# Causal maxima of the first attention scores: the mask moves from TensorE's products to VectorE's maxima

## The reference

```
attn = jnp.einsum('bqhd,bkhd->bhqk', q, k) * scale
causal = jnp.tril(jnp.ones((S, S), dtype=bool))
attn = jnp.where(causal, attn, jnp.float32(-jnp.inf))
attn = jax.nn.softmax(attn, axis=-1)
out = jnp.einsum('bhqk,bkhd->bqhd', attn, v).reshape(B, S, C)
```

## Time and profile before

| | us |
|---|---|
| timed runs, median (lowest, highest) | 3667.57 (3660.76, 3667.74) |
| the profiled execution, its own time | 3655.43 |
| its span, on which all times below count | 3653.7 |
| TensorE busy over the span | 3193.2 (87%) |
| VectorE busy over the span | 2187.1 (60%) |
| ScalarE busy over the span | 1428.5 (39%) |
| mask products of the first scores, L2572 | 512 |
| maxima, L2664 | 128, 188.0 us busy |

### The profile page before, as it was taken

How to read it: one execution, slowest core, us unless ns; L and a number is a source line. 1 busy time by engine, 2 the same in 40 slices (tenths; PEclk the granted TensorE clock), 3 DMA queues, 4 the chain that set the end, 5 groups by cost and what they waited for, 6 DMA issues and landing times.

```text
span 3653.7 us, 86956 instructions
## 1 busy us (share of the span) xinstructions
PE 3193.2 (87%) x35518; PEld 2230.1 (61%) x35518; DVE 2187.1 (60%) x4820; ACT 1428.5 (39%) x3328; POOL 936.6 (26%) x851
## 2 busy tenths in 40 slices
PE   5689988888988888898868889776999999999998
PEld 5367665666666666666757767665545555554553
DVE  7566777566678666678346645635435545545444
ACT  1534443444443444344136622134433433333241
POOL 0112221412222512231406536341221231220110
PEclk7898998898998989899679989898989999999999
DMA  6111210411111301211348755384111111111000
GB/s 238 41 36 46 65 44 28 128 32 60 51 52 48 122 20 54 60 51 35 100 151 204 183 157 144 103 285 145 23 43 45 47 35 47 41 30 41 1 18 18
DMA packets 224087, 280.89 MB, mean 77 GB/s; under 512 B 35072, under 2 KB 172464, under 8 KB 223312
## 3 DMA queue, kind: packets, MB, share of 16 engines
q1 hardware_dynamic: 184448, 216.93, 18.4%
q0 software_dynamic: 34896, 54.20, 6.7%
q10 hardware_dynamic: 4352, 4.20, 0.3%
HBM read 184.64 MB, written 90.62 MB: 75 GB/s over the span
## 4 chain that ended last, share of the span: by engine, by line
PE 67%; DVE 16%; ACT 5%; issue 4%; DMA 3%; POOL 2%; DVEq 0%; ACTq 0%; SPq 0%; POOLq 0%
PE banks L3020 6%; PE banks L570 5%; DVE s_d_kq L663 4%; PE banks L2586 3%; PE banks L1936 3%; PE banks L2570 2%; PE banks L1278 2%; PE banks L806 2%; PE banks L1945 2%; PE banks L2598 2%; PE banks L966 2%; PE banks L2738 2%; PE banks L794 2%; PE banks L2828 2%; PE banks L964 2%
## 5 line engine op out<-in xcount | busy, mean ns | idle before, releaser
L570 PE MATMUL banks<-s_d_xT,s_w_qkvg 128*128 128x512 f32 x640 | 342.0, 661 | 15.9 <-DVE s_d_kq L663 11.4
L663 DVE SCALAR_TENSOR_TENSOR s_d_kq<-banks,s_conv_w,s_d_kq 128x511 f32<-128x511 f32 (+2 forms) x384 | 286.0, 745 | 49.9 <-ACT s_d_kq L615 40.3
L2700 ACT ACTIVATE s_g_pT<-banks 128x1536 f32<-128x1536 f32 (+1 forms) x96 | 152.8, 1591 | 361.0 <-PE banks L2588 361.0
L2664 DVE TENSOR_REDUCE s_g_nmax<-banks 128x4 f32<-128x512 f32 (+3 forms) x128 | 188.0, 1490 | 162.8 <-PE banks L2572 162.8
L3020 PE MATMUL banks<-s_m_we,s_m_tT 128*128 128x512 f32 x512 | 235.0, 604 | 8.1 <-DVE s_m_x L3084 7.8
L641 ACT ACTIVATE s_d_square<-banks 128x128 bf16<-128x128 f32 x512 | 134.0, 275 | 161.5 <-PE banks L599 161.5
L570 PEld LDWEIGHTS banks<-s_d_xT,s_w_qkvg 128*128 128x128 f32 x640 | 125.8, 208 | 115.8 <-issue 89.4
L615 ACT ACTIVATE s_d_kq<-banks,s_conv_w 128x512 f32<-128x512 f32 x128 | 87.8, 686 | 271.1 <-PE banks L570 270.5
L1936 PE MATMUL banks<-s_q_xsT,s_q_w 128*128 x1008 | 159.9, 282 | 38.4 <-issue 27.5
L1936 PEld LDWEIGHTS banks<-s_q_xsT,s_q_w 128*128 128x128 f32 x1008 | 153.7, 196 | 61.1 <-issue 49.1
L806 PEld LDWEIGHTS banks<-s_d_TB,s_d_XT 32*32 32x32 f32 x9216 | 111.1, 112 | 89.0 <-issue 41.9
(11 more groups left out here) (411 smaller groups left out, 7588.1 us busy)
## 6 DMA issues: line engine op xcount, KB each, us to landing
s_q_w<-w12p SPq DMA_DIRECT2D x128, 257.0 KB, 6.3
s_q_xs<-xs SPq DMA_DIRECT2D x32, 516.0 KB, 6.4
s_d_E<-sums SPq DMA_DIRECT2D x64, 256.0 KB, 3.6
s_r_xT<-xfT SPq DMA_DIRECT2D x12, 1024.0 KB
tree<-s_r_bias SPq DMA_DIRECT2D x96, 128.0 KB, 2.2
s_r_work<-xf SPq DMA_DIRECT2D x24, 512.0 KB, 4.4
og<-s_d_o SPq DMA_DIRECT2D x16, 512.0 KB, 3.0
sorted<-s_q_acc SPq DMA_DIRECT2D x32, 256.0 KB, 2.1
```

What stands on the lines that cost most here:

```text
L570: ins = e.matmul(bk[6 + j % 2][:], w[:, par, c, self.COL[what] + h * P:self.COL[what] + (h + 1) * P], xT[:, c, :], start=(c == 0), stop=(c ...
L663: e.scalar_tensor_tensor(d[:, a:], bk[6 + j % 2][:, 0:SEQ - a], cw[:, par, k0 + 3 - a:k0 + 4 - a], d[:, a:], ALU.mult, ALU.add).then_inc(s ...
L2664: e.tensor_reduce(self.nmax[:, t, :].rearrange("p (k d) -> p k d", k=4)[:, :, 16], psum[:, 0:4, a:a + (t + 1) * P], AX.X, ALU.max, negate= ...
L2700: e.activation(self.pT[c][:], psum[:, 0:4, 0:self.COLUMNS[c]], ACT.Exp).then_inc(self.exped, 1)
```

## The change

The four mask products of a tile go away; the score products close their group themselves. VectorE gets a new tile `off` with one maximum for each head, and a semaphore `off_made`. For tiles 1 to 3 it reduces the 128 t columns left of the diagonal block into `off`, for all four heads at once. Then, for each head of each tile, one `tensor_tensor_reduce` adds the mask to the diagonal block, writes the sum back over the block in PSUM, and takes its maximum, starting from `off` (from -1e30 in tile 0), into `nmax`. `nmax` now has the maximum's own sign, so the queries' addition becomes a subtraction. An unused set of semaphores is dropped.

```diff
@@ -2567,9 +2568,7 @@
         for t, a in self.MAXIMA[u]:
             W = (t + 1) * P
             for k in range(4):
-                ins = e.matmul(bk[k][:, a:a + W], qkT[32 * k:32 * k + 16, j, t * P:(t + 1) * P], qkT[32 * k:32 * k + 16, 4, 0:W], start=True, stop=False, skip_group_check=True)
-            for k in range(4):
-                ins = e.matmul(bk[k][:, a + t * P:a + (t + 1) * P], self.g.identb[:], self.g.neglb[:], start=False, stop=True, skip_group_check=True)
+                ins = e.matmul(bk[k][:, a:a + W], qkT[32 * k:32 * k + 16, j, t * P:(t + 1) * P], qkT[32 * k:32 * k + 16, 4, 0:W], start=True, stop=True, skip_group_check=True)
         ins.then_inc(self.scored, 1)
@@ -2661,7 +2660,16 @@
                     for t, a in units:
-                        e.tensor_reduce(self.nmax[:, t, :].rearrange("p (k d) -> p k d", k=4)[:, :, 16], psum[:, 0:4, a:a + (t + 1) * P], AX.X, ALU.max, negate=True).then_inc(self.maxed, 1)
+                        if t:
+                            e.tensor_reduce(self.off[:, t, :], psum[:, 0:4, a:a + t * P], AX.X, ALU.max).then_inc(self.off_made, 1)
+                    for t, a in units:
+                        if t:
+                            e.wait_ge(self.off_made, 3 * (m + 1) + t)
+                        for k in range(4):
+                            block = g.bank[k][:, a + t * P:a + (t + 1) * P]
+                            lower = self.off[:, t, k:k + 1] if t else -1e30
+                            ins = e.tensor_tensor_reduce(block, block, g.neglb[:], 1.0, lower, ALU.add, ALU.max, self.nmax[:, t, 32 * k + 16:32 * k + 17])
+                        ins.then_inc(self.maxed, 1)
@@ -2684,7 +2692,7 @@
                     e.wait_ge(self.max_turned, m + 2)
-                    e.tensor_tensor(q, turns[:], q, ALU.add).then_inc(self.q_made, 1)
+                    e.tensor_tensor(q, q, turns[:], ALU.subtract).then_inc(self.q_made, 1)
```

More of the change, by code:

```diff
@@ L71, in __init__ @@
         self.stored = [self.sems(f"side_store{n}") for n in range(4)]
-        self.on_tensor, self.on_vector, self.on_scalar, self.on_gpsimd = (self.sems("side_" + n) for n in ("tensor", "vector", "scalar", "gpsimd"))
+        self.on_tensor, self.on_vector, self.on_scalar = (self.sems("side_" + n) for n in ("tensor", "vector", "scalar"))
     def sem(self, name):
@@ L2315, in __init__ @@
         self.oT, self.rden = sb("g_oT", [P, SEQ]), sb("g_rden", [P, TPB, 4])
+        self.off, self.off_made = sb("g_off", [P, TPB, 4]), g.sem("second_off_made")
         self.at, self.aoT = two("g_at", [P, TPB, DIM]), sb("g_aoT", [P, KC, 256])
```

## The result

In the comparison that goes with the forecast the changed kernel took 3639.41 us (median of 5 runs) against 3660.76 of the kernel before (5 runs): ratio 0.9942, 95% interval 0.9923 to 0.9961. Two later comparisons gave 0.9997 [0.9966, 1.0027] and 0.9974 [0.9954, 0.9994]. The three differ among themselves by more than their intervals allow, so a mean of them says little: by whole times the change is worth something between nothing and 0.6%. The sign rests on the stage itself.

What follows compares the result with a forecast made beforehand. TensorE was taken as the bound. Masks saved 34 us, steady-stretch waits for longer maxima cost 34, the ends 8 and the clock 2: +10 us on 3667.57, so 3677.6 us, range 3649 to 3725 (8 in 10).

Steps and rivals of the forecast that it cites:

- The bound: Second layer's stage: TensorE, busy 1047.12 of 1103.70 us, sets the pace; its saved work saves time unless another engine is late.
- The masks: TensorE's mask products: 128 groups at 0.33 us; 4.3 us a stretch remain, 34 us over eight, give or take 13.
- The price of the pair: VectorE's pass plus read-out for each head: 0.34 us start to start, bounded by 0.27 and 0.49.
- rival 1: VectorE's pair is short, 0.27 us: stalls of 2.0 us a stretch, kernel 12 us faster, 3655; chance 0.25.
- The waits: TensorE waiting for longer maxima in six units of a steady stretch: 4.2 us a stretch, 34 us over eight.
- Ends: Waits for maxima ahead of the first exponentials, in the first round A and near the end: +8 us.
- The clock: Longer waits around the low-clock stretch in the stage's first round A: 2 us added to the sum.
- Rival 3: Clock falls in the steady stretches too, 2.5 us in each of eight, 20 us on top: 3698; chance 0.11.
- The median: Whole kernel: +10 us added to the earlier median of 3667.57 us, giving 3677.6.

Runs made afterwards that it cites:

- E1: The kernel before without its 512 mask products, old maxima kept, causal mask left out of them: ratio 0.9962 to before, steady stretch 128.81 us.
- E2: The changed kernel with the 512 mask products put back on TensorE, so VectorE's part alone: ratio 1.0086 to before, steady stretch 134.20 us.
- E7: The changed kernel with one of a tile's four mask products left in: single time 3657.5 us, stretch 131.87 us without a fall of the clock.
- E9: The changed kernel with the head-wise pass made one without a maximum read-out: one execution 3648.89 us, steady stretch 129.55 us.
- E6: The changed kernel with a small 128x1 copy ahead of each of the 512 pairs: ratio 1.0055 to before.
- E8: The changed kernel with masks and single reduces kept in the first round, rounds A's unit 0 and rounds C's unit 2: ratios 0.9972 and 0.9949 to before.
- E5: The changed kernel with the pass of tiles 1 to 3 writing into the neighbour head's bank: one execution 3671.75 us, steady stretch 130.20 us.

## Why the prediction was wrong

**The bound, right.** TensorE sets the pace; what is taken off it counts except where VectorE comes last. E1 and E2 show both halves.

**The masks, too dear by a fifth.** The term was 0.33 a group, 5.28 us a stretch and 4.3 after 0.99 was taken off for A0 and D2. Measured: 0.18 for a single group, 0.72 for unit 0's two, 4.3 for all sixteen and 3.21 in E1, where A0 and the new wait for GpSimd take their share. No row of the trace before said that the 3.49 behind four masks would become 3.63; that took the changed kernel, and its cause E7. The range of 0.1 a group either way held it. Put right alone, this term would have made the forecast slower still.

**The price of the pair, the step that failed.** "My value is the sum nearest to a row: 0.27 + 0.07 = 0.34." Measured 0.27, and 0.25 with a constant, the low bound and rival 1's value. Rival 1's number is partly luck: it was made up of a pass of 0.20 and a read-out of 0.07, and with the scalar, as in three of four pairs, the pass alone takes 0.26 (E9). Both rows were read rightly: L759's 0.27 is a pass with a scalar (0.26 in E9), and a small instruction costs 0.07 (E6's copy adds 0.06 to 0.07). But two overheads that each stand in a row by themselves were added, the scalar's 0.06 and the read-out's 0.05, and together they cost 0.07. Of the 0.07 by which 0.34 was too high, 0.04 is this overlap (0.20 + 0.06 + 0.05 = 0.31 against 0.27); the rest is the pass taken at 0.27 for 0.26 and the read-out at 0.07 for 0.05. So the maxima grew by 0.94 (0.60 + 4 x 0.25 + 4 x 0.27 + 0.08 = 2.76 against 1.82) and by about 0.66 in units 1 and 2, not by 1.59, 0.94 and 0.95. At 0.33 to 0.34, in E6, the steady stretch has 0.3 us of its gain left and the kernel was slower as a whole, so this step decides whether there is a gain at all.

**The waits, right in place, too long by that step.** Forecast 4.2 us a stretch in A0, B0, C0, C2, D0 and B2; measured 0.24 in B0, 0.33 in C2, 0.61 + 0.11 on the two sides of A0, on top of the masks lost there, and about 0.16 in D0, where the 0.94 meets a gap of 0.75 and the 0.15 that TensorE now loses behind the scores. B2 had none: B2-C0 has its whole 0.73. Rival 1's list (1.03, 0.33, 0.39, 0.28) is the better one. Over the whole stage TensorE's waits for the maxima went from 19.1 to 37.3 us, 18 more; the forecast had 42 (34 and 8) and rival 1 22.

**Ends.** Forecast +8 for the waits there. The table of stretches doesn't part them from the masks saved; with both, the first rounds are 0.9 us shorter, the two intervals between the A rounds at either side of the steady ones 3.1 and 0.8, and the last rounds the same. In the first round A the three waits for the maxima went from 3.28, 1.40 and 2.39 us to 5.12, 2.03 and 3.16, 3.2 more where the forecast had 1.9; what they cost is within these numbers. The forecast also counted eight steady stretches. The trace has five from A0 to A0, 662.1 us before and 653.0 after, and they bring 9.1 of the 13.9 us of the first two profiles.

**The clock.** Rival 3 was at work, at a smaller size: 1.7 us in one or two stretches of five, where one fall (in C0-C1) stood before, against 2.5 us in each of eight. In E6 it is the larger part of the 13 us that the stage lost.

**The median.** Forecast 3677.6, measured 3639.41. Of the 38 us between, 7 lie in the kernel before, which took 3660.76 in this comparison and not the 3667.57 on which the sum was built; the other 31 are +10 against -21. Rival 1 gave -12 us; the profiled stages say -11 to -14, the medians -21, +3 and -10, so the -21 holds some 7 us that are not the change's. The chance of 0.25 for it was low: its value was one of two bounds, and with the trace's own evidence for overlap the case between 0.27 and 0.31 deserved as much as the sum.

## What to carry to other kernels

Price a train of small instructions by the distance from start to start of the nearest row as a whole; overheads taken from different rows (a scalar, a small extra instruction) may share the same time, as they did here, and then their sum is an upper bound and not the middle. Where a change trades TensorE's time for VectorE's, list for each unit of work the gap between the end of the one and the start of the other: a growth up to the gap is free, beyond it it counts, unless the engine would have waited there for a third one anyway (C2 and GpSimd). The exchange can be made unit by unit (E8, for the steady stretch). Removed products give back less than their own time where they had paid for a change of tile shape that the next product must now pay.

## What the runs showed of the hardware

- VectorE: a pass over 128x128 out of PSUM with two tensors follows the next at 0.20 us, with a scalar from memory at 0.26, with an accumulator read-out at 0.25, with both at 0.27, while one lasts 0.29 to 0.36 (changed kernel and E9). An extra copy of 128x1 adds 0.06 to 0.07 (E6). Writing the result into the PSUM bank being read or into another makes no difference (355 ns either way, E5).
- TensorE: behind score products of 16 rows the first product over 128 rows pays for the change, 0.10 us if it is a mask product (0.16 against 0.06) and 0.14 to 0.15 in what stands there without masks (E7 and E1). The change back costs too: the second tile's scores take 0.64 us behind masks and, by difference, 0.44 behind scores.
- TensorE's clock: behind waits of 1.1 us the granted clock was 0.53 (1.2 instead of 2.4 GHz) for 3.4 us, which costs 1.7 us, in some repetitions of the same code and not in others (2, 1 and 2 of 5 in three profiles).
- The same code ahead of the stage ended anywhere within 31 us in one execution each on the first chips (2541.6 to 2572.9): a difference of 0.3% in whole times wants the stage's own time beside it.
